# Two-layer graph network on one core: first projection started block by block, and softmax denominators summed on GpSimd

## What is computed

```python
# layer 0: GAT with 8 heads of 768, then one head
h = (x @ W1).reshape(n, 8, 768)                       # W1 is 768 x 6144
alpha_s, alpha_d = (h * a_src).sum(-1), (h * a_dst).sum(-1)
e = exp(leaky_relu(alpha_s[src] + alpha_d[dst]) - segment_max)
out = segment_sum(h[src] * e, dst) / segment_sum(e, dst) + b
h = elu(out); second GAT layer with W2 (6144 x 768), one head
x = layernorm(x + that)
# layer 1: two GCN layers (768 x 768), relu between
x = layernorm(x + that)
```

## Time and profile before

| what | value |
|---|---|
| median of 3 runs | 1658.85 us (1658.64 to 1658.88) |
| profiled execution | 1656.4 us, its span 1654.6 us |
| PE busy | 1630.6 us, 99% of the span |
| DVE, ACT, POOL busy | 1234.6, 770.0, 155.7 us |
| mean granted PE clock | 0.997 of full |

### The profile page before, as it was taken

One profiled execution on the slowest core, in us unless ns is written; L12 is line 12 of the kernel. 1 busy time (PEld: TensorE's weight loads), 2 busy tenths in 40 slices (PEclk: granted clock), 3 DMA queues, 4 the chain that ended last, 5 costly groups with the idle time before them and its releaser, 6 DMA issues. The chain is left out here.

```text
span 1654.6 us, 21905 instructions
## 1 busy us (share of the span) xinstructions
PE 1630.6 (99%) x7552; PEld 1368.2 (83%) x7552; DVE 1234.6 (75%) x2442; ACT 770.0 (47%) x1231; POOL 155.7 (9%) x126
## 2 busy tenths in 40 slices
PE   7999999999999999999999999999999999999998
PEld 6878888888878888888888888888888888989898
DVE  7877667655988788788778788877886668785447
ACT  3222223222565565456555555655564435644340
POOL 1211232322200000000000000000000001031003
PEclk9999999999999999999999999999999999999999
DMA  7444555984647475558647565754754447023222
GB/s 258 161 156 156 162 193 190 242 214 151 223 172 184 170 210 153 131 188 226 155 152 200 156 167 187 200 143 164 200 140 172 178 163 195 21 94 97 66 96 88
DMA packets 135331, 271.86 MB, mean 164 GB/s; under 512 B 24234, under 2 KB 83508, under 8 KB 122676
## 3 DMA queue, kind: packets, MB, share of 16 engines
q1 hardware_dynamic: 133968, 267.26, 52.9%
q0 software_dynamic: 1152, 3.15, 1.0%
q10 hardware_dynamic: 100, 0.03, 0.0%
HBM read 210.01 MB, written 60.40 MB: 163 GB/s over the span
## 5 line engine op out<-in xcount | busy, mean ns | idle before, releaser
L41 PE MATMUL psum<-ph,hc 128*128 128x512 f32 x768 | 299.4, 390 | 2.2 <-DVE pl L1040 1.2
L42 PE MATMUL psum<-pl,hc 128*128 128x512 f32 x768 | 298.8, 389 | 0.0
L43 PE MATMUL psum<-ph,hc 128*128 128x512 f32 x768 | 298.8, 389 | 0.0
L41 PE MATMUL psum<-wh,xTh 128*128 128x512 f32 x570 | 226.3, 397 | 0.4 <-issue 0.4
L42 PE MATMUL psum<-wl,xTh 128*128 128x512 f32 x570 | 222.2, 390 | 0.0
L43 PE MATMUL psum<-wh,xTl 128*128 128x512 f32 x570 | 222.0, 389 | 0.0
L979 DVE CUSTOM_DVE_ANT_0 junk<-psum,a_bc 128x512 bf16<-128x512 f32 (+1 forms) x256 | 129.8, 554 | 118.6 <-ACT st L623 108.6
L623 ACT CAST st<-psum 128x512 fp32r<-128x512 f32 x96 | 56.4, 588 | 296.2 <-PE psum L43 285.3
L41 PEld LDWEIGHTS psum<-ph,hc 128*128 128x128 f32 x768 | 144.2, 188 | 33.9 <-DVE pl L1040 2.1
L43 PEld LDWEIGHTS psum<-ph,hc 128*128 128x128 f32 x768 | 144.2, 188 | 30.0
L42 PEld LDWEIGHTS psum<-pl,hc 128*128 128x128 f32 x768 | 144.2, 188 | 29.7
(11 more groups left out here) (285 smaller groups left out, 3116.7 us busy)
## 6 DMA issues: line engine op xcount, KB each, us to landing
hc<-h_scratch SPq DMA_DIRECT2D x96, 1024.0 KB, 5.3
h_scratch<-st SPq DMA_DIRECT2D x96, 512.0 KB, 3.2
w2r<-in_L_gnn_W SPq DMA_DIRECT2D x96, 384.0 KB, 6.8
wr<-in_L_gnn_W SPq DMA_DIRECT2D x12, 1536.0 KB, 8.6
gwr<-in_L_gnn_W SPq DMA_DIRECT2D x24, 384.0 KB, 3.4
row_bc<-logits_scratch SPq DMA_DIRECT2D x16, 512.0 KB, 12.9
expo_bc<-expo_scratch SPq DMA_DIRECT2D x16, 512.0 KB, 6.2
xr<-in_x SPq DMA_DIRECT2D x2, 1536.0 KB, 10.2
```

The costliest lines, as they stand in the source:

```text
L41: nc.tensor.matmul(out, sh, mh, start=first, stop=False, skip_group_check=not grouped)
L42: nc.tensor.matmul(out, sh, ml, start=False, stop=False, skip_group_check=not grouped)
L43: return nc.tensor.matmul(out, sl, mh, start=False, stop=last, skip_group_check=not grouped)
```

## The change

Three parts, and an order that joins them.

1. Denominators. For units 1 to 15 the two matmuls, ACT's copy and DVE's low part are gone. POOL runs one `partition_all_reduce` of `psum_rows` (128x512) into the new tile `den`, and `inverse(u, den)` moves from the end of unit u - 1 into unit u, behind `exponents` and ahead of `average`. Unit 0 is as before.
2. Start. `x` is loaded in four DMAs (block 0, blocks 1 and 2, 3 and 4, 5 to 7), W1's first chunk in three; `turn_x(b)` now turns one node block (six transposes into banks 6 and 7). Block 0 is turned first, block 1 inside step 0, block b behind step b - 2. POOL copies two of the six high parts of the first chunk. Eleven matmuls on a zeroed tile (`stay_warm`) stand around block 0's transposes. The edges are loaded on ACT's queue, and the small vectors on SP's.
3. Order. DVE makes block 0's low part and W1's six low parts, and only then the keys; PE turns the keys behind step 1 and the bias columns behind step 2; DVE's `bounds` stands behind step 1. In steps 1 to 7 the six matmuls with x's low part come last. `hot(w)` stands behind step w + 3 and `count(w)` behind step w + 5; `count(0)` waits for all of x's low parts, since banks 6 and 7 hold turned blocks till then. A transposition of logits moves from (4, 4) to (4, 5).

```diff
+XR0 = 3
+X_PARTS = ((0, 4), (4, FB))
+WARM, STAY_WARM = 8, 3
...
-    X_AFTER = {0: range(FB, FB + 4), 1: range(FB + 4, XG)}
-    HOT_AT = {w + 1: w for w in range(NW)}
-    COUNT_AFTER = {w + 3: w for w in range(NW)}
+    X_AFTER = {b - 2: b for b in range(2, NB)}
+    W0_POOL_HIGH, W0_ACT_HIGH = (1, 3), (0, 2, 4, 5)
+    W0_DVE_LOW = tuple(range(FB))
+    HOT_AT = {w + 3: w for w in range(NW)}
+    COUNT_AFTER = {w + 5: w for w in range(NW)}
...
+            for f in W0_POOL_HIGH:
+                pool.wait_ge(w0_in[f // 2], 16)
+                nc.gpsimd.tensor_copy(wh[0][:, f, :], wr[0][:, f, :]).then_inc(w0_pool, 1)
...
+            for v in range(1, U):
+                pool.wait_ge(p_sum, 7 * v + 7)
+                pool.wait_ge(rden_done, v)
+                if v == H + 1:
+                    pool.wait_ge(rows_saved[1], 16)
+                nc.gpsimd.partition_all_reduce(den[:, :], psum_rows[:, :], channels=P, reduce_op=bass.bass_isa.ReduceOp.add).then_inc(den_full, 1)
...
+            def x_low(b):
+                for i, (lo, hi) in enumerate(X_PARTS):
+                    dve.wait_ge(x_hi, 2 * b + i + 1)
+                    bs = slice(b * P, (b + 1) * P)
+                    nc.vector.tensor_tensor(xTl[:, lo:hi, bs], x_turn(i), xTh[:, lo:hi, bs].bitcast(F32), ALU.subtract).then_inc(x_lo, 1)
...
                 if u >= 1:
+                    inverse(u, den)
                     second_low(g + 1)
                 average(g)
...
+            def turn_x(b):
+
+                x_arrived(pe, b)
+                if b >= 1:
+                    pe.wait_ge(x_lo, 2 * b)
+                part = xr[0][:, b, :] if b < XR0 else xr[1][:, b - XR0, :]
+                for i, (lo, hi) in enumerate(X_PARTS):
+                    for f in range(lo, hi):
+                        last = nc.tensor.matmul(banks[6 + i][:, (f - lo) * P:(f - lo + 1) * P], part[:, f * P:(f + 1) * P], ident[:, :],
+                                                start=(f == lo), stop=(f == hi - 1), is_transpose=True, skip_group_check=True)
+                    last.then_inc(x_turned, 1)
...
+            stay_warm(WARM)
             pe.wait_ge(const_g, 5)
...
+            turn_x(0)
+            stay_warm(STAY_WARM)
...
-                if w >= 2:
+                if w == 0:
+                    pe.wait_ge(x_lo, 2 * NB)
+                elif w >= 2:
                     pe.wait_ge(count_out, w - 1)
...
+                    elif n < NB:
+                        pe.wait_ge(x_hi, 2 * (n + 1))
+                        for f in range(FB):
+                            nc.tensor.matmul(banks[n % 6][:, :], xTh[:, f, bs], wh[0][:, f, :], start=(f == 0), stop=False)
+                            nc.tensor.matmul(banks[n % 6][:, :], xTh[:, f, bs], wl[0][:, f, :], start=False, stop=False)
+                        pe.wait_ge(x_lo, 2 * (n + 1))
+                        for f in range(FB):
+                            last = nc.tensor.matmul(banks[n % 6][:, :], xTl[:, f, bs], wh[0][:, f, :], start=False, stop=(f == FB - 1))
...
-                if v < U:
-                    pe.wait_ge(a_out, u * FB + FB - 1)
-                    sum_weights(v, banks[6])
```

## The result

The changed kernel takes 1649.3 us (median of 4 runs, 1647.02 to 1649.71) against 1658.74 (4 runs): ratio 0.9940, 95% interval [0.9923, 0.9958], which is 9.4 us less. The forecast was 1647.8 with a range from 1643.5 to 1653.0. Nearly all of the gain comes from the denominators. In the profiled execution (1649.59 us) the start had won over 7 us by step 5 and gave them back ahead of step 6.

A forecast was written before the change was run, and what follows sets the result against it. PE, busy 99% of the span, was taken as the bound. Denominators 7.0 plus start 4.0 made 11.0 us off 1658.85, giving 1647.8 us, with a range from 1643.5 to 1653.0.

The forecast's parts named there:

- What bounds the kernel: Whole kernel: PE busy 99% of the span, so only fewer or faster matmuls or shorter PE waits move the time.
- Fifteen pairs at 0.47 us, 7.0: Attention units: fifteen pairs of matmuls with ones leave PE, 0.47 us each, 7.0 us gained in full.
- The reduction, taken as 11.7 us and hidden: Attention units: POOL's reduction in seven passes, 11.7 us, below the 18 us free, so it costs nothing.
- Rival 4: Attention units: reduction outlasts its cover; over 22.5 us on POOL holds PE at each unit's third gather; chance 0.05.
- The instruction with a page's 247.7 us: POOL's reduction: another instruction's page figure, quartered to 62 us, would hold PE up by about 590 us.
- The two ISA rows on POOL at nothing: POOL, ahead of the first reduction and ahead of `cl`: two new ISA rows, counted as costing nothing.
- Step 0 ends 10.7 us sooner: Start: step 0 over at 13.0 us against 23.7, a lead of 10.7 us.
- The lead shrinks by 0.6 (transposes up to step 5), 0.7, 0.7 and 0.9: Behind step 0: transposes 1.25 in all, keys and columns 0.7, block 2's wait 0.7, W1's second chunk 0.9 us.
- The wait of `count(0)`, 3.2 us: Behind step 5: PE waits 3.2 us for block 7's low part, behind ACT's copy and DVE's work.
- The clock in it: In the wait of `count(0)`: granted clock forecast to stay at 1.00.
- rival 1: Clock falls in the new wait, earlier fall cost about 2.6 us; start gives 1.4 us, total 1650.4; chance 0.24.
- 4.0 forecast: Start's net gain: the 10.7 us lead less 1.25, 0.7, 0.7, 0.9 and 3.2, leaving 4.0 us.

The follow-up runs named there:

- the run with three: Changed kernel with hot and count one step later, GpSimd's reduction of each unit done three times over: 1642.88 us, ratio 0.9914.
- the run with five: Changed kernel with hot and count one step later, GpSimd's reduction of each unit done five times over: 1669.03 us, one execution.
- the start alone: Changed kernel with the denominators back on TensorE, start and order as changed: 1656.17 us, ratio 0.9993.
- the kernel with the filled wait: Changed kernel with thirteen multiplications of zeros put between block 7's transposes and the first count: 1646.64 us, ratio 0.9937.

## Why the prediction was right, and where it wasn't

The sign and the side that gives the most were right, and the median lies 1.5 us from the forecast. Two errors in the sum are part of that closeness: the denominators gave more than they were put at, and the start less.

- **What bounds the kernel.** Right: PE is busy for 99% in both kernels, and the time moved by PE's work, PE's waits and PE's clock.
- **Fifteen pairs at 0.47 us, 7.0.** Mis-sized, measured 7.4 in the distance of the units (0.49 each) and 8.1 with the wait in unit 8 that vanished. The list of waits had that wait at 0.3 us and it wasn't in the sum. (That list also has 1.2 us for `pl` in the attention, which the prediction doesn't name; both kernels have it.) The attention's 8.1 us are less than the 9.4 by which the medians differ, and what the rest is, is open.
- **The reduction, taken as 11.7 us and hidden.** It takes 3.87 us, between the bounds of 1.68 and 213 and nearer to the lower. "Hidden" was right, and nearly so at 10.7 us (the run with three, 1.35 us). The reason given, 18 us free and 22.5 before PE waits, was wrong in kind: it treated VectorE's exponents as fixed, and the run with five shows PE waiting at 17.4 us because they aren't. Rival 4's threshold of 22.5 us was therefore too high.
- **The instruction with a page's 247.7 us.** The estimate of 62 us from the Trainium skill ("GPSIMD Engine Reference", section 3.2) is not borne out for this instruction: 3.87 us.
- **The two ISA rows on POOL at nothing.** Right for the time. Ahead of the first `cl` POOL now idles 6.8 us, in no row of its own, hidden by the 111.3 us in which its next work waits for a DMA. The Trainium skill ("GPSIMD Engine Reference", section 2.1) gives some 6 us for the first call to freshly loaded code; the 6.8 us are near that. What the engine does in them no row shows.
- **Step 0 ends 10.7 us sooner.** 9.5 to 9.9: the transposes that follow begin at 14.18 and not 13.0, since W1's parts land and are copied later than reckoned (the last high products begin at 9.51 us).
- **The lead shrinks by 0.6 (transposes up to step 5), 0.7, 0.7 and 0.9.** 7.8 us was to be left at step 5, and 7.7 is what the copies show. In the parts the errors cancel: block 2's transposes wait 0.2 and not 0.7 us, and W1's second chunk, copied by ScalarE at 24.54 us after 3.8 us of waiting (forecast 25), costs PE no wait at all.
- **The wait of `count(0)`, 3.2 us.** 3.1 by the timeline. The chain of a copy, VectorE's work of step 5 and the low part is what stood there: 39.95 to 42.79 us.
- **The clock in it.** This is the step that failed. The forecast took "no fall", on the ground that the wait is shorter than the one in the earlier trace rows and PE had been busy before it. It fell, 0.9 us behind the end of the wait and in the traces of both kernels that have this order and an unfilled wait (the changed one and the start alone), and cost 2.7 us, the 2.6 that rival 1 had; that rival had been given 0.24. One thing wasn't in any case: the gap of 0.9 us behind the loop. The account closes: 4.0 forecast, less 2.7 and 0.9, is 0.4, and -0.1 is what the trace shows.
- **Multiplying the low part last, and the keys behind the low parts.** The prediction had no term for them, and the runs show none (within 0.4 us each).

With rival 1's start (1.4 us) and 7.0 the forecast would have been 1650.4; with the gap of 0.9 and the denominators' 8.1 it is 1650.2, less than 1 us above the median.

The executions of one kernel differ by more than these terms. A second place where the clock falls is part of that, the passage from the attention to the second layer. There the changed kernel, in the profiled execution, has

```profile
1370.00:1380.00 10.00, 7.25 (x27) 0.75 1.07 260
```

and the kernel with the filled wait, in its own,

```profile
1360.00:1370.00 10.00, 7.91 (x40) 1.00 1.01 343
1370.00:1380.00 10.00, 7.49 (x36) 1.00 1.08 208
```

That one was the fastest of its five, 1645.24 us, 1.4 below their median. Whether this place or the first makes the changed kernel's run of 1647.02 us isn't shown, since one execution has a trace. What stays open is also how short a wait must be for the clock to hold. No fall was seen without a wait, and the wait of 3 us was tried at one length only. But in the passage to the second layer much shorter ones were enough: the changed kernel's fall comes at 1375.0 us behind waits of 1.62 and 0.56 us, and in the kernel with the filled wait the same two waits left the clock at 1.00. So the same waits can go either way, and the fall at `count(0)` is shown in the two traced executions, not in every one.

## What to carry to other kernels

A lead won at the start is only as good as the first place where another engine's chain meets it: follow the lead in the trace by one row a step, find the step where it goes, and move the work that waits, here by one step for 7.0 us in the traces (the copies at step 40). Price a wait of TensorE of about 3 us with the half clock behind it (here 2.7 us), not by its length alone. When work moves to GpSimd beside a full VectorE, the cover must be counted through VectorE's own queue, since the two can stop each other, and an operation that another engine waits for can be the one that is stretched.

## What the runs showed of the hardware

- After 25 us in which TensorE was busy with hardly a gap came a wait of 3.1 us, 0.9 us of matmuls and a second gap of 0.85 us; the granted clock fell to 0.50 at the start of that second gap. With zeros multiplied in the wait and the second gap as it was, it kept 1.00, and the difference was 2.7 us.
- `partition_all_reduce` of 128x512 float32 took 3.23 us where none of VectorE's longer operations was under way at its start. It took 3.43 us where the low part of W2 (`w2l`, two inputs in SBUF) ended 0.33 us after that start, and 3.87, the length in the changed kernel, where it ended 0.77 us after it.
- VectorE's operations with two inputs in SBUF are held up by such a reduction in turn: 128x1024 passes take 3.26 to 3.28 us instead of 1.23. In the runs with five and three, passes that start with a reduction end 0.09 us behind its end, and stretched 128x512 operations end 0.45 us ahead of it; counted back by their usual length, both get going 1.1 us before the reduction ends. `he` starts 1.08 to 1.14 us before that end in most units and keeps its 0.69 us; where it starts 1.4 us before it (two units of the run with three) it takes 0.95. `mean`, with one input in PSUM, kept 0.69 us at any point. In the changed kernel no such operation starts in the part that holds VectorE up. The Trainium skill ("SBUF — State Buffer", "Who interferes with whom") says that a VectorE instruction with two SBUF inputs contends with a GpSimd instruction that reads SBUF, and calls the shared port pair an exclusive lock. The rows agree on which operations contend; for this reduction they show VectorE held up until 1.1 us before its end, not to the end.
- The column of the granted clock reads 1.00 from the first window on also where single matmuls take the time of half clock: the eight multiplications of zeros are 0.43 us apart in the changed kernel. At the very start of a program the durations tell the clock, not that column.
